# Half of the last attention placed between the second experts' products, in a four-layer transformer kernel

## The chip, the cores and the metric

The kernel runs on one core of a Trainium2 chip, as one program. The metric is the device time of that program in microseconds. A core has five engines that run side by side, each working through its own queue in order and waiting only for semaphores: TensorE (PE in the profile; its weight loads are PEld), VectorE (DVE), ScalarE (ACT), GpSimd (POOL), and SyncE (SP), which issues transfers. Matmul results land in PSUM, eight banks of 128 x 512 numbers; everything else lies in SBUF.

## What is computed

Four layers, each a cross-attention and a feed-forward, on x of 16 x 64 tokens with 128 features (1024 tokens, 8 tiles of 128). Every part reads the normalised x and adds its result to x. The part that matters here:

```python
x = x + L2_xattn(ctx, ctx, layernorm(x))          # deformable attention
x = x + L2_ffn(layernorm(x))                      # experts; only tokens 0..511 are routed
x = x + L3_xattn(layernorm(x), ctx, ctx, mask, bias)
x = x + L3_ffn(layernorm(x))

# L2_ffn: 8 experts, 128 -> 512 -> 128, two picked per token
h = gelu(ragged_dot(xs, w1, tokens_per_expert)); ys = ragged_dot(h, w2, tokens_per_expert)
out = zeros.at[tok].add(ys * weight) + bias

# L3_xattn: 16 heads of 8
q, k, v = clamp(Q @ Wq.T + bq), clamp(K @ Wk.T + bk), clamp(V @ Wv.T + bv)
logits = q @ k.T / sqrt(8) + clip(attn_bias, -1e4, 1e4)
logits = where(mask == 0, -1e4, logits)
x_add = softmax(logits) @ v @ Wo.T + bo

# L3_ffn: values rounded to a step of (largest of |v|) / 32767, five times one after the other
act_qdq(v) = clip(round(v / scale), ...) * scale,  scale = max(max|v| / 32767, 1e-12)
```

The expert picks come as inputs. Tokens 512 to 1023 get only the bias from L2_ffn, so after the deformable attention their x is complete up to that bias. The scale in act_qdq is the largest value of the whole tensor.

## The kernel before

There is no loop construct: the program is written out, engine by engine, in the order in which each queue runs it. "Tile j" is tokens 128 j to 128 j + 127.

*Deformable attention* (`deformable`, lines 1415 to 1936) works through 16 steps w. At its start ScalarE evacuates the offsets in two halves, and between them the two halves of the last layer's keys (lines 1550 to 1554), whose product TensorE has made at line 1389. VectorE then turns the first offsets to positions (`positions`, a chain of about 13 linked operations), GpSimd the other three quarters. At its end tokens 0 to 511 are finished first: context projection (w = 15), addition, statistics, and `HalfNorm`, a layernorm of one half of the tokens (lines 322 to 386). Tokens 512 to 1023 are finished between the experts (`late_half_pe`, `late_half_act`, `late_half_dve`).

*Second experts* (`moe2`, lines 1956 to 2033). For each of 8 experts TensorE makes four up products into PSUM banks 0 to 3 (line 2003), ScalarE applies GELU to each (line 2032), TensorE makes 16 down products into bank 4 or 5 by turns (line 2014), and VectorE adds the result, weighted per token, to x (line 1983, four instructions). TensorE's order is up(e + 1), down(e). Besides: the last layer's key guard (clamping; `guard`, lines 432 to 443), value products (line 492), value evacuation (line 457) and guard, key expansion to one copy per head group (line 451, VectorE), value spreading (line 481, ScalarE), and the limited bias, eight tiles (line 2093).

*Last attention* (`attention`, lines 507 to 739, masked). It begins when all x is done: layernorm of 8 tiles, query product in two halves (line 535), evacuation (543), guard of the queries, then 8 tiles in order 0 to 7. For a tile: scores on TensorE (585), times scale and plus limited bias on VectorE (686, 689), maximum (692), minus the maximum on GpSimd (667), exponential on ScalarE (645), clearing of NaN on VectorE (712), eight transposes on TensorE (599) and their evacuation on ScalarE (652), weighing of values and sums (612, 616), division on VectorE (718, 719, 723), output projection (636), addition (729) and statistics (251). TensorE runs scores one tile ahead and weighing two tiles behind.

*Last feed-forward* (`ffn3`, lines 2124 to 2327). Five times a largest value over all partitions is found and made a scale (`all_max`, lines 2156 to 2166), on which rounding on ScalarE and VectorE waits. The output leaves in two halves (line 2337).

`dve_link` makes VectorE wait for its own instruction; `stay_busy` issues matmuls whose result nobody reads.

## Time and profile before

| | us |
|---|---|
| time, median of 3 runs (502.0 to 504.98) | 503.25 |
| profiled execution, its own time | 501.5 |
| its span in the profile | 499.7 |
| TensorE busy (matmuls) | 398.9 |
| VectorE busy | 362.5 |
| ScalarE busy | 231.6 |
| GpSimd busy | 110.8 |

The span is from the first to the last instruction of the profiled execution; 1.8 us of its time lie around it. Busy times overlap, since the engines run side by side. The clock that TensorE was granted was 0.903 of full speed on average; it has two levels, 2.4 GHz (1.00) and 1.2 GHz (0.50).

### The profile page before, as it was taken

The numbers are of one execution on the slowest core, as the hardware profiler recorded it, in microseconds if no ns is written. First come the engines' busy times: TensorE is split into PE (matmuls) and PEld (weight loads), VectorE is DVE, ScalarE is ACT, GpSimd is POOL, SyncE is SP. The second block draws the span as 40 slices with busy tenths as digits, with TensorE's granted clock in tenths as the row PEclk, the third lists the DMA queues.
The fourth block names the chain that finished last, engine by engine and source line by source line (L and its number), as shares of the span: only waits on it lengthen the run. The fifth ranks groups of instructions, "written<-read, shape, count | busy, mean of one in ns | idle before, by whom it ended". The sixth has DMA issues, their size and how long they took to land.

```text
span 499.7 us, 8507 instructions
## 1 busy us (share of the span) xinstructions
PE 398.9 (80%) x3345; PEld 262.8 (53%) x3345; DVE 362.5 (73%) x806; ACT 231.6 (46%) x405; POOL 110.8 (22%) x95
## 2 busy tenths in 40 slices
PE   4998899999999887847888858999947386778155
PEld 2566565666566675623545434777742254653045
DVE  4889647567455779667788875198985999776974
ACT  3655663243222453437887857231712233343931
POOL 3100000009930010059925442000001343100000
PEclk9879999999999999988999987999976579679769
DMA  7960000000000000350000020000000000000001
GB/s 250 356 234 3 1 1 1 1 0 1 0 1 1 1 3 0 127 212 1 1 1 3 1 63 1 0 2 1 1 1 0 0 2 3 1 1 1 0 0 42
DMA packets 11068, 16.49 MB, mean 33 GB/s; under 512 B 5259, under 2 KB 9749, under 8 KB 10133
## 3 DMA queue, kind: packets, MB, share of 16 engines
q1 hardware_dynamic: 10740, 15.17, 8.6%
q10 hardware_dynamic: 288, 0.79, 0.4%
q8 instruction: 26, 0.43, 0.4%
q14 instruction: 14, 0.11, 0.1%
HBM read 15.43 MB, written 0.52 MB: 32 GB/s over the span
## 4 chain that ended last, share of the span: by engine, by line
PE 48%; DVE 35%; ACT 9%; issue 6%; DMA 1%; POOL 0%; ACTq 0%; DVEq 0%
PE ps L894 7%; PE ps L899 7%; PE ps L933 6%; PE ps L2003 4%; PE ps L2014 3%; PE ps L585 2%; DVE arena L689 2%; PE ps L1703 2%; DVE arena L686 2%; DVE arena L692 2%; PE ps L241 2%; DVE stats L251 2%; PE ps L1689 2%; PE ps L599 1%; DVE l2buf L2093 1%
## 5 line engine op out<-in xcount | busy, mean ns | idle before, releaser
L1012 DVE SCALAR_TENSOR_TENSOR arena<-ps,cols,arena 128x512 f32<-128x512 f32 x40 | 29.7, 750 | 42.3 <-PE ps L899 38.0
L908 ACT ACTIVATE arena<-ps,cols 128x512 f32<-128x512 f32 x40 | 27.4, 687 | 63.9 <-PE ps L894 63.8
L1838 DVE TENSOR_SCALAR arena<-ps 128x512 f32<-128x512 f32 x56 | 36.7, 684 | 10.0 <-PE ps L1689 5.6
L933 PEld LDWEIGHTS ps<-weights,arena 128*128 128x128 f32 x320 | 38.6, 192 | 8.1 <-issue 8.0
L933 PE MATMUL ps<-weights,arena 128*128 128x128 f32 x320 | 39.2, 276 | 0.2 <-DVE x_tm L1001 0.2
L899 PE MATMUL ps<-h_fm,weights 128*128 128x512 f32 x80 | 37.7, 594 | 0.7 <-DVE arena L1012 0.7
L894 PE MATMUL ps<-h_fm,weights 128*128 128x512 f32 x80 | 37.7, 594 | 0.6 <-ACT h_fm L382 0.6
L241 PE MATMUL ps<-const 128*128 128x256 f32 x114 | 29.9, 415 | 8.4 <-ACT arena L2243 4.6
L645 ACT ACTIVATE arena<-arena 128x1024 f32<-128x1024 f32 x16 | 16.9, 1057 | 37.3 <-POOL arena L667 29.9
L2003 PE MATMUL ps<-h_fm,weights 128*128 128x512 f32 x64 | 31.4, 639 | 0.7 <-ACT h_fm L382 0.7
L2014 PEld LDWEIGHTS ps<-weights,arena 128*128 128x128 f32 x256 | 29.7, 192 | 3.3 <-issue 3.1
L1689 PE MATMUL ps<-l2buf,picks_b 128*128 128x256 bf16 x160 | 26.9, 289 | 5.1 <-DVE arena L1838 3.7
L241 PEld LDWEIGHTS ps<-const 128*128 128x128 f32 x114 | 22.8, 208 | 14.5 <-ACT arena L2243 4.9
L599 PE MATMUL ps<-const,arena 128*128 128x128 f32 x128 | 23.1, 340 | 9.0 <-DVE arena L712 9.0
L2014 PE MATMUL ps<-weights,arena 128*128 128x128 f32 x256 | 29.7, 275 | 0.0
L2032 ACT ACTIVATE arena<-ps 128x512 f32<-128x512 f32 x32 | 18.6, 594 | 22.3 <-PE ps L2003 22.2
L585 PE MATMUL ps<-kexp,q_fm 32*64 32x256 f32 x256 | 25.5, 472 | 3.8 <-DVEq L552 1.9
L599 PEld LDWEIGHTS ps<-const,arena 128*128 128x128 f32 x128 | 18.7, 176 | 15.0 <-DVE arena L712 9.8
L667 POOL TENSOR_TENSOR arena<-arena 128x1024 f32<-128x1024 f32 x8 | 17.9, 2237 | 36.3 <-DVE arena L692 36.3
L899 PEld LDWEIGHTS ps<-h_fm,weights 128*128 128x128 f32 x80 | 15.1, 190 | 20.2 <-issue 18.2
L1703 PE MATMUL ps<-arena,kexp 128*32 128x320 f32 x256 | 20.5, 438 | 5.6 <-ACT l2buf L1784 4.1
L652 ACT ACTIVATE arena<-ps 128x512 f32<-128x512 f32 x32 | 17.9, 594 | 14.3 <-PE ps L599 14.3
(352 smaller groups left out, 837.3 us busy)
## 6 DMA issues: line engine op xcount, KB each, us to landing
weights<-in_moe_w SPq DMA_DIRECT2D x2, 2048.0 KB, 10.1
weights<-in_moe_w SPq DMA_DIRECT2D x3, 1280.0 KB
l2buf<-in_picks SPq DMA_DIRECT2D x1, 1664.0 KB, 7.5
rows<-in_rows SPq DMA_DIRECT2D x1, 1024.0 KB, 13.7
x_tm<-in_x SPq DMA_DIRECT2D x2, 256.0 KB, 4.9
ctx_fm<-in_ctx_fm ACTq DMA_DIRECT2D x1, 512.0 KB, 5.6
ctx_tm<-in_ctx SPq DMA_DIRECT2D x1, 512.0 KB, 14.5
mats<-in_mats SPq DMA_DIRECT2D x1, 512.0 KB, 14.6
```

The source lines that it names most:

```text
L241: PE.matmul(ps[:, bank, 0:256], ident, const[:, 0:256], start=True, stop=True)
L585: ins = PE.matmul(ps[64 * b:64 * b + 64, 2 * (t % 2) + g % 2, 256 * (g // 2):256 * (g // 2) + 256], q_fm[32 * g:32 * g + 32, t * P + 64 * ...
L599: ins = PE.transpose(ps[:, 4 + k, 128 * c:128 * c + 128], prob[j % 3][:, (4 * k + c) * 128:(4 * k + c + 1) * 128], ident)
L894: PE.matmul(ps[:, k, :], w1[:, e, P * k:P * k + P], h_fm[:, t], start=True, stop=True)\
L899: PE.matmul(ps[:, 2 + k, :], w2[:, e, P * k:P * k + P], h_fm[:, t], start=True, stop=True)\
L933: ins = PE.matmul(ps[:, 4 + u % 2, P * t:P * t + P], glu[:, u % 2, k, P * t:P * t + P], w3[:, e, k, :], start=(k == 0), stop=(k == 1))
L1012: V.scalar_tensor_tensor(out=glu[:, u % 2, k, :], in0=ps[:, 2 + k, :], scalar=bias_col(1, e, k), in1=silu[:, k, :], op0=ALU.add, op1=ALU.m ...
L1689: ins = PE.matmul(ps[:, m % 3, 256 * i:256 * i + 256], picks_b[:, 2 * c + i, :], ixm[:, hg, 256 * half:256 * half + 256], start=True, stop ...
L1703: ins = PE.matmul(ps[32 * hl:32 * hl + 32, 4 + par, 0:NK * S], kvc[:, j, 4 * hg + hl, :], hats[:, u % 2, NK * hl:NK * hl + NK, S * (2 * i ...
L1838: V.tensor_scalar(hat_rows(u, c), ps[:, m % 3, :], 0.0, 1.0, ALU.max, ALU.min).then_inc(near_ok, 1)
L2003: PE.matmul(ps[:, k, :], m2w1[:, e, P * k:P * k + P], h_fm[:, 0:T2], start=True, stop=True)\
L2014: ins = PE.matmul(ps[:, 4 + e % 2, P * j:P * j + P], hid[:, e % 2, k, P * j:P * j + P], m2w2[:, e, k, :], start=(k == 0), stop=(k == 3))
```

## The change

1. The last layer's keys are evacuated at the end of `int8_linear` and guarded before `positions`; its values are multiplied at the end of `deformable` (banks 0, 1, 2, 4) and evacuated there.
2. `last_keys_values`, `moe2` and the last call of `attention` are replaced by one function, `experts_and_last_attention`. In it up products rotate over three banks, down products use the single bank 3, tokens 512 to 1023 are normalised after accumulate(0), tiles 7, 6, 5 are attended between the experts, and tile 4 and then 3, 2, 1, 0 after them. ScalarE expands the keys. The limited bias is computed tile by tile. The output projection is done for groups of four, two, one and one tiles.
3. In `ffn3` the scale of each rounding is a step times a unit, so that the reciprocal follows the step directly; the output is in pieces of four, two and two tiles.

The helper functions inside the new function (scores, turn, weigh_values, logits, clear_nan, divide and so on) hold the same instructions as the old lines named above, for one tile.

```diff
--- before.py
+++ after.py
...
+        def keep_last_keys(act):
+
+            for k in range(2):
+                act.wait_ge(l3_keys[0], k + 1)
+                AC.activation(k_fm[:, 512 * k:512 * k + 512], ps[:, k, :], ACT.Identity,
+                              bias=col("L3_xattn_b_k")).then_inc(l3_keys[1], 1)
+
+        def guard_last_keys(dve):
+
+            dve.wait_ge(l3_keys[1], 2)
+            guard(k_fm[:], T, (l2buf[:, 5632:6656], l2buf[:, 6656:7680], wn[:].rearrange("p c i -> p (c i)")[:, 0:1024]))
+            keys_guarded.append(chained["dve"])
...
+        def keep_last_values(dve, g):
+
+            dve.wait_ge(v_ps, g + 1)
+            V.tensor_tensor(vdup[:, g], ps[:, VALUE_BANKS[g], :].rearrange("p (b e) -> p b e", b=4),
+                            over(row("L3_xattn_b_v"), 1, 4), ALU.add).then_inc(v_sb, 1)
...
+                keep_last_keys(act)
 
         int8_linear(3)
...
-                    if g == 0:
-                        for k in range(2):
-                            act.wait_ge(l3_keys[0], k + 1)
-                            AC.activation(k_fm[:, 512 * k:512 * k + 512], ps[:, k, :], ACT.Identity,
-                                          bias=col("L3_xattn_b_k")).then_inc(l3_keys[1], 1)
...
             def _(dve):
+                guard_last_keys(dve)
                 positions(dve, V, dve_link, 0, slice(0, 4), parts_ok)
...
                     if w == 15:
                         project_context(pe, 0, 3)
+                        last_values(pe, 0)
+                    if w == 16:
+                        last_values(pe, 1)
+                last_values(pe, 2)
+                last_values(pe, 3)
+                stay_busy(pe, 3, 5)
                 late_norm.turn(pe, 3)
...
                     if w == 16:
                         add_context(dve, 0, 3)
                         late_norm.moments(dve)
+                for g in range(4):
+                    keep_last_values(dve, g)
                 normalise(3)
...
+        def experts_and_last_attention():
...
+            TILES = (7, 6, 5, 4, 3, 2, 1, 0)
+            LATE = 4
+            GROUPS = ((4, 8), (2, 4), (1, 2), (0, 1))
+            GROUP_END = (4, 6, 7, 8)
...
+            SUM_BANK, O_BANK, Y_BANK = 3, 7, 3
+            early_rows, late_rows = HalfNorm(1), HalfNorm(0)
+
+            def score_banks(t):
+
+                return (0, 1) if t >= LATE and t % 2 == 0 else (4, 5)
+
+            def turn_banks(t):
+
+                return (2, 6) if t >= LATE else (6, 6)
...
+                def up(e):
+                    for k in range(4):
+                        n = 4 * e + k
+                        if n >= 3:
+                            pe.wait_ge(g_ok, n - 2)
+                        else:
+                            pe.wait_ge(v_sb, n + 1)
+                        PE.matmul(ps[:, n % 3, :], m2w1[:, e, P * k:P * k + P], h_fm[:, 0:T2], start=True, stop=True)\
+                            .then_inc(up_ps, 1)
+
+                def down(e):
+                    pe.wait_ge(g_ok, 4 * e + 4)
+                    if e >= 1:
+                        pe.wait_ge(sum_added, e)
+                    for j in range(4):
+                        for k in range(4):
+                            ins = PE.matmul(ps[:, SUM_BANK, P * j:P * j + P], hid[:, e % 2, k, P * j:P * j + P],
+                                            m2w2[:, e, k, :], start=(k == 0), stop=(k == 3))
+                    ins.then_inc(sum_ps, 1)
...
+                    j, banks = TILES[t], score_banks(t)
+                    if t == 0:
+                        pe.wait_ge(kx_ready, 1)
+                        pe.wait_ge(v_sb, 4)
+                        pe.wait_ge(q_ok, 1)
+                    if t == LATE:
+                        pe.wait_ge(kx_ready, 2)
+                        pe.wait_ge(q_ok, 2)
+                    for g in range(4):
+                        if g < 2 and t >= 1 and t != LATE:
+                            before = t - 1 if t < LATE else t - 2
+                            pe.wait_ge(sc_read, 2 * before + g + 1)
+                        if g >= 2:
...
+                def turn(t, k):
+                    if k == 0:
+                        pe.wait_ge(clean, t + 1)
+                    if t < LATE:
+                        if t + k >= 1:
+                            pe.wait_ge(pt_ready, 2 * t + k)
+                    elif t > LATE or k == 1:
+                        pe.wait_ge(pt_ready, 2 * (t - 1) + k + 1)
+                    for c in range(4):
+                        ins = PE.transpose(ps[:, turn_banks(t)[k], 128 * c:128 * c + 128],
+                                           prob[t % 3][:, (4 * k + c) * 128:(4 * k + c + 1) * 128], ident)
+                    ins.then_inc(ptT_ready, 1)
...
+                late_norm.wait_turned(pe)
+                pe.wait_ge(moe2_in, 64)
+                up(0)
+                up(1)
+                turn_late_context(pe, 6)
+                down(0)
+                project_late_context(pe, 7)
+                up(2)
+                down(1)
+                early_rows.turn(pe, 6)
+                up(3)
+                early_rows.wait_turned(pe)
+                queries(1, 7)
+                down(2)
+                scores(0)
+                up(4)
+                down(3)
+                scores(1)
+                up(5)
+                turn(0, 0)
+                down(4)
+                turn(0, 1)
+                up(6)
+                weigh_values(0)
+                turn(1, 0)
+                down(5)
+                turn(1, 1)
+                scores(2)
+                up(7)
+                down(6)
+                weigh_values(1)
+                turn(2, 0)
+                down(7)
+                scores(3)
+                turn(2, 1)
+                stay_busy(pe, 3, 2)
+                late_rows.turn(pe, 0)
+                weigh_values(2)
+                late_rows.wait_turned(pe)
+                queries(0, 1)
+                stay_busy(pe, 4, 2)
+                turn(3, 0)
+                turn(3, 1)
+                scores(4)
+                scores(5)
+                for t in range(5, NT + 3):
+                    if t + 1 < NT:
+                        scores(t + 1)
+                    if t - 2 < NT:
+                        weigh_values(t - 2)
+                    if t - 1 < NT:
+                        turn(t - 1, 0)
+                        turn(t - 1, 1)
+                    if t == 6:
+                        project(0)
+                    if t == 8:
+                        project(1)
+                    if t == 9:
+                        project(2)
+                    if t == 10:
+                        project(3)
...
+                pool.wait_ge(def_cx_ok, 2)
+                G.memset(v4[:], 0.0).then_inc(cleared, 1)
+                early_rows.wait(pool)
+                add_out_bias(slice(4, 8))
+                less_max(0)
+                less_max(1)
+                less_max(2)
+                late_rows.wait(pool)
+                add_out_bias(slice(0, 4))
+                for t in range(3, NT):
+                    less_max(t)
...
+                V.tensor_scalar(bqs[:, 1:2], col("L3_xattn_b_q"), 1.0, None, ALU.mult).then_inc(bq_ok, 1)
+                expert_gates()
+                late_norm.wait(dve)
+                dve_link(V.tensor_tensor(x_tm[:, 0:4], x_tm[:, 0:4], over(row("L2_ffn_bias"), 1, 4), ALU.add))
+                limits()
+                accumulate(0)
+                add_late_context(dve, 7)
+                early_rows.moments(dve)
+                limited_bias(0)
+                early_rows.factors(dve)
+                early_rows.apply_on_dve(dve, (0, 1))
+                guard_values(1)
+                accumulate(1)
+                limited_bias(1)
+                guard_queries(0, 1)
+                accumulate(2)
+                logits(0)
+                limited_bias(2)
+                accumulate(3)
+                logits(1)
+                clear_nan(0)
+                accumulate(4)
+                guard_values(0)
+                clear_nan(1)
+                limited_bias(3)
+                divide(0)
+                limited_bias(4)
+                accumulate(5)
+                logits(2)
+                limited_bias(5)
+                dve.wait_ge(vx_ready, 8)
+                limited_bias(6)
+                accumulate(6)
+                clear_nan(2)
+                limited_bias(7)
+                accumulate(7)
+                dve.wait_ge(sum_added, NE)
+                all_stats(range(0, 4))
+                late_rows.moments(dve)
+                divide(1)
+                late_rows.factors(dve)
+                late_rows.apply_on_dve(dve, (0, 1))
+                logits(3)
+                guard_queries(1, 0)
+                divide(2)
+                clear_nan(3)
+                logits(4)
+                for t in range(5, NT + 5):
+                    if t < NT:
+                        logits(t)
+                    if t - 1 < NT:
+                        clear_nan(t - 1)
+                    if 3 <= t - 3 < NT:
+                        divide(t - 3)
+                    if t == 7:
+                        add(0)
+                    if t == 8:
+                        add_stats(0)
+                    if t == 9:
+                        add(1)
+                    if t == 10:
+                        add(2)
+                        add_stats(1)
+                    if t == 11:
+                        add(3)
+                        add_stats(2)
+                    if t == 12:
+                        add_stats(3)
+                V.sem_inc(x_done, 1)
...
+                                            k_fm[:, 512 * k:512 * k + 512].rearrange("p (b k) -> p b k", b=8), ACT.Copy,
+                                            scale=const[:, C_HM + h:C_HM + h + 1])
+                    ins.then_inc(kx_ready, 1)
+
+                def spread_values(half):
+                    act.wait_ge(v_sb, 6 - half)
+                    act.wait_ge(cleared, V4_CLEAR_AGAIN)
+                    for part in range(4):
...
+                gelu(0)
+                gelu(1, (0, 1))
+                keep_late_context(act)
+                gelu(1, (2, 3))
+                keep_turned_late_context(act, 6)
+                spread_keys(1)
+                gelu(2)
+                early_rows.root(act)
+                early_rows.apply_on_act(act, (2, 3))
+                early_rows.keep_turned(act, 6)
+                gelu(3)
+                keep_queries(0, 1, 7)
+                spread_values(1)
+                gelu(4)
+                spread_keys(0)
+                exponential(0)
+                gelu(5)
+                keep_turned(0, 0)
+                exponential(1)
+                keep_turned(0, 1)
+                gelu(6)
+                keep_turned(1, 0)
+                spread_values(0)
+                keep_turned(1, 1)
+                gelu(7)
+                exponential(2)
+                keep_turned(2, 0)
+                late_rows.root(act)
+                keep_turned(2, 1)
+                late_rows.apply_on_act(act, (2, 3))
+                late_rows.keep_turned(act, 0)
+                keep_queries(1, 0, 1)
+                exponential(3)
+                keep_turned(3, 0)
+                keep_turned(3, 1)
+                for t in range(LATE, NT + 1):
+                    if t < NT:
+                        exponential(t)
+                    if t - 1 >= LATE:
+                        keep_turned(t - 1, 0)
+                        keep_turned(t - 1, 1)
+
+        experts_and_last_attention()
...
+            def set_unit(dve, i, ins):
+
+                dve_link(ins)
+                dve_link(V.reciprocal(least[:, i:i + 1], unit[:, i:i + 1]))
+                dve_link(V.tensor_scalar(least[:, i:i + 1], least[:, i:i + 1], 1e-12, None, ALU.mult))
+
             def all_max(dve, i):
 
 
                 dve.wait_ge(all_ps, i + 1)
                 dve_link(V.tensor_reduce(top, ps[:, 7, 0:P], AX.X, ALU.max))
-                dve_link(V.tensor_scalar(scl[:, i:i + 1], top, real[:, i:i + 1], 1e-12, ALU.mult, ALU.max))
-                dve_link(V.reciprocal(inv[:, i:i + 1], scl[:, i:i + 1]))
-
-                V.scalar_tensor_tensor(out=inv[:, i:i + 1], in0=inv[:, i:i + 1], scalar=32767.0, in1=real[:, i:i + 1],
-                                       op0=ALU.mult, op1=ALU.mult).then_inc(scale_ok, 1)
+                dve_link(V.tensor_scalar(step[:, i:i + 1], top, 1.0 / 32767.0, least[:, i:i + 1], ALU.mult, ALU.max))
+                V.reciprocal(inv[:, i:i + 1], step[:, i:i + 1]).then_inc(scale_ok, 1)
                 dve.wait_ge(scale_ok, i + 1)
+
+            def full_scale(i):
+
+                return V.tensor_tensor(scl[:, i:i + 1], step[:, i:i + 1], unit[:, i:i + 1], ALU.mult)
...
-                for k in range(2):
-                    for j in range(4 * k, 4 * k + 4):
+                for k, (j0, j1) in enumerate(PIECES):
+                    for j in range(j0, j1):
                         if j % 2 == 0:
...
                 for i in (GT, UP):
-                    ins = V.tensor_scalar(real[:, i:i + 1], scl[:, X:X + 1], 1.0 / 32767.0, None, ALU.mult)
-                dve_link(ins)
+                    set_unit(dve, i, V.tensor_copy(unit[:, i:i + 1], step[:, X:X + 1]))
...
                     if c == 0:
                         all_max(dve, UP)
+                        dve_link(full_scale(UP))
                     dve.wait_ge(dve_chain, product)
...
                 all_max(dve, GT)
-                V.tensor_scalar(real[:, GS:GS + 1], scl[:, GT:GT + 1], 1.0 / 65536.0 / 32767.0, None, ALU.mult)
+                dve_link(full_scale(GT))
...
+                set_unit(dve, GS, V.tensor_scalar(unit[:, GS:GS + 1], scl[:, GT:GT + 1], 1.0 / 65536.0, None, ALU.mult))
...
+                dve_link(full_scale(GS))
+                set_unit(dve, OUT, V.tensor_tensor(unit[:, OUT:OUT + 1], scl[:, GS:GS + 1], scl[:, UP:UP + 1], ALU.mult))
...
+                dve_link(full_scale(OUT))
+                for k, (j0, j1) in enumerate(PIECES):
...
+        PIECES = ((0, 4), (4, 6), (6, 8))
+        ffn3(5)
...
-            for k in range(2):
+            for k, (j0, j1) in enumerate(PIECES):
                 sp.wait_ge(halves_done, k + 1)
-                sp.dma_start(out.rearrange("(j p) d -> p j d", p=P)[:, 4 * k:4 * k + 4], x_tm[:, 4 * k:4 * k + 4])\
-                    .then_inc(out_done, 16)
-            sp.wait_ge(out_done, 32)
+                sp.dma_start(out.rearrange("(j p) d -> p j d", p=P)[:, j0:j1], x_tm[:, j0:j1]).then_inc(out_done, 16)
+            sp.wait_ge(out_done, 16 * len(PIECES))
...
```

## Rows read from the trace of the kernel before

**Rows 1.** Page, busy tenths of each engine in 40 slices of 12.5 us.

```profile
PE   4998899999999887847888858999947386778155
DVE  4889647567455779667788875198985999776974
```

**Rows 2.** Windows: start:end, length, busy us of PE, PEld, DVE, ACT, POOL, clock, DMA.

```profile
300.30:302.30 2.00, 1.16 (x5) 0.76 (x5) 0.86 (x2) 0.78 (x3) 0.00 (x0) 0.50 0.03 8
302.30:369.90 67.60, 64.23 (x396) 46.66 (x396) 49.45 (x89) 27.51 (x57) 3.51 (x1) 0.95 0.00 1
369.90:380.90 11.00, 5.59 (x12) 2.75 (x12) 5.80 (x25) 5.13 (x9) 2.36 (x1) 0.59 0.00 0
380.90:442.20 61.30, 39.67 (x592) 27.21 (x592) 54.24 (x85) 18.98 (x27) 17.90 (x8) 0.71 0.01 1
```

**Rows 3.** Chain that ended last: start us, us on it, what.

```profile
302.26 9.57 PE ps L2003 x16
...
322.84 0.89 PE ps L1649 x8
323.74 3.44 PE ps L2003 x8
327.17 3.57 PE ps L2014 x32
330.74 1.90 PE ps L492 x32
...
342.58 0.69 DVE l2buf L439
...
345.77 1.38 DVE l2buf L443
...
405.78 1.29 DVE arena L686 x2
```

**Rows 4.** Timeline, 200 to 334: start us, us, engine, line, names [idle before].

```profile
215.96 0.42 DVE L1568 TENSOR_TENSOR o_fm<-o_fm,const 128x256 f32<-128x256 f32 x1 [6.14 <-ACT o_fm L1548]
...
218.12 0.75 DVE L1573 TENSOR_TENSOR o_fm<-o_fm,sinv 128x256 f32<-128x256 f32 x1
...
300.46 1.11 PE L376 MATMUL ps<-const,h_tm 128*128 128x128 f32 x4 [4.21 <-ACT h_tm L358]
...
303.87 1.28 ACT L2032 ACT_TABLE_LOAD   x1
303.88 0.44 DVE L1881 TENSOR_REDUCE v<-v 128x32 f32<-128x160 f32 x1 [2.69 <-ACT v L1778]
...
305.16 0.60 ACT L2032 ACTIVATE arena<-ps 128x512 f32<-128x512 f32 x1
...
333.37 4.48 DVE L451 TENSOR_TENSOR kexp<-k_fm,const 128x2048 f32<-128x2048 f32 x2
```

**Rows 5.** Timeline of the last attention.

```profile
386.47 2.12 DVE L440 TENSOR_SCALAR ctx_tm<-q_fm 128x512 f32<-128x512 f32 x1
...
409.91 1.42 PE L585 MATMUL ps<-kexp,q_fm 32*64 32x256 f32 x16
...
410.41 0.95 DVE L719 RECIPROCAL arena<-arena 128x128 f32<-128x128 f32 x1
...
434.56 0.68 PE L612 MATMUL ps<-arena,v 128*32 128x64 f32 x31 [0.46 <-ACT arena L652]
...
435.07 0.64 PE L616 MATMUL ps<-arena,const 128*32 128x128 f32 x15
435.64 1.09 PE L599 MATMUL ps<-const,arena 128*128 128x128 f32 x8
```

**Rows 6.** Timeline of the last feed-forward.

```profile
468.49 0.16 DVE L2164 SCALAR_TENSOR_TENSOR arena<-arena 128x1 f32<-128x1 f32 x1
...
479.45 1.22 DVE L2310 SCALAR_TENSOR_TENSOR arena<-arena 128x1024 f32<-128x1024 f32 x1 [1.11 <-ACT arena L2243]
...
496.21 0.75 DVE L2325 SCALAR_TENSOR_TENSOR x_tm<-ps,arena,x_tm 128x512 f32<-128x512 f32 x1 [1.93 <-PE ps L2202]
```

463 lines of the change are left out of this document (239 added, 224 removed).

## The prediction

> **What bounds the kernel now.** The profile page comes first. In its 40 slices TensorE is dense and VectorE looser in slices 25 to 29, the second experts; in slices 31 to 35, the last attention, they change places [rows 1]. The stage windows put numbers on it [rows 2]. Experts, 302.3 to 369.9: TensorE busy 64.2 of 67.6 us, VectorE 49.5. Turn-over (layernorm, queries) to 380.9: 11.0 us in which neither is busy for much over half. Last attention to 442.2: VectorE 54.2 of 61.3, TensorE 39.7, much of that at a lower clock. So these are two stages one behind the other with different limits. Over both, 139.9 us, VectorE works 109.5 us and TensorE 109.5 us. The chain of waits says the same: TensorE up and down products with VectorE's accumulations at the end, then only VectorE logits [rows 3]. Tokens 512 to 1023 need no second experts, so their attention can fill VectorE's gaps there; tokens 0 to 511 can't, which is why it is half of the attention that moves.
>
> The timing is played through: four queues kept in order, durations from rows, each wait looked up.
>
> **Part by part: ahead of the experts.** Key evacuation moves to ScalarE's idle time before 207.9, the key guard to VectorE's idle 6.1 us before 215.96 [rows 4]. The guard is five operations, 342.58 to 347.15 = 4.6 us [rows 3]; it starts at 209.8 and ends at 214.4, so it costs nothing, with 1.5 us of cover left; without cover 4.6. The second offset evacuation then comes 1.3 us sooner, so GpSimd starts sooner beside VectorE's position chain, which is on the path. A product or sum of two 128x256 tiles took 0.42 us at 215.96 with GpSimd idle and 0.75 at 218.12 with it busy [rows 4]. Two or three more operations are caught: +0.6 (0 to 1.3).
>
> The first value product now lies between the context projection and the next turn on TensorE, on the chain: two groups of values take 1.90 us [rows 3], so +0.95. The other three and the stay-busy products fill TensorE's 4.2 us of idle before 300.46 [rows 4]. VectorE's four value evacuations, 4 x 0.69, fall where it waits 2.7 us for the exponential [rows 4], and the first up products wait for them, to 302.8, 303.6 and 304.3. The first GELU comes at 305.5 instead of 305.16 and there are three banks instead of four, so up(0) and up(1) end by GELU's pace at 310.5; before they ended at 311.8, since they ran at 1.2 GHz (granted 0.50 at 300.3 to 302.3 [rows 2], 9.57 us for 16 records, at full speed 2 x 3.44 [rows 3]). down(0) starts at 310.9: 0.7 us earlier.
>
> **Experts with three tiles inside.** TensorE's order from down(0) to the end of down(7): 8 downs x 3.57, 6 ups x 3.44, context projection 0.89 [rows 3], a turn of the norm 0.45, half the queries 0.86, scores of tiles 0 to 2 at 1.42, two weighings at 1.15, five half turns at 0.45 (eight transposes show 1.09, of which 0.2 is the last one's run-out) [rows 5]: 28.6 + 20.6 + 0.9 + 0.45 + 0.86 + 4.3 + 2.3 + 2.25 = 60.2. Without a stall down(7) would end at 371.2. With the queues in order I find these waits of TensorE: 0.5 for the norm rows, 1.6 for accumulate(1) (one sum bank; VectorE is in the value guard), 0.6 for guarded queries, 0.9, 1.6 and 0.9 for the cleared tiles 0, 1 and 2, and 0.5 of scraps: 6.6. down(7) ends at 377.8 and accumulate(7) at 379.1, against 369.8 before: the stage is 9.3 longer. VectorE has 109.5 less 4.5 (key expansion) less 4.6 less 2.8 (now ahead) = 97.6 us from 308.4 [rows 2 to 4], a floor of 406, so it can't be the bound before the late tiles.
>
> ScalarE takes the key expansion as 8 activations at 0.64 (the nearest row is a 128x512 GELU at 0.60 [rows 4]; a scale from a tile may add; bounds 0.60 and 0.75), 5 us. From the experts on it switches function tables 10 times instead of 3: GELU and exponential alternate. A switch costs 1.28 us: at 303.87 the load starts with the end of the exponential and GELU starts 0.01 us after it [rows 4]. 7 x 1.28 + 5 on 51.6 busy makes 66 of 130 us; most of it hides behind down products. The Trainium skill (ScalarE: Activation LUTs, "What ACT_TABLE_LOAD costs") adds a drain of about 1.38 us to each load and so budgets some 2.7 per switch, with the advice to group by table; this trace shows no such gap. By the page's price, played through the same queues, the end would come 6.5 us later, the sum would be 499.0.
>
> **Turn-over and the late tiles.** From accumulate(7): statistics, root and normalised rows 4.1 us, to 383.2; logits(3) 4.1; the query guard 4.9, since GpSimd's subtraction holds it up (0.42 became 2.12 at 386.47 [rows 5]); divide(2) and clear_nan(3) 2.2, to 394.4. By then TensorE has idled some 7 us, so its clock is low, as it was through much of the old attention (0.71 on average [rows 2]); two half turns and the scores of tile 4 take 4.1 before VectorE can start logits(4) at 398.5. From there it is the old loop: before, 405.78 to 442.2 = 36.5 from the first logits of tile 4 [rows 3]. Two of the seven divisions in it (reciprocal 0.95 [rows 5], 1.46 with the two small steps around it) are done already: 33.5. x_done comes at 432.0, against 442.2: **-10.2**.
>
> **Last layer.** Each scale drops one linked operation of 0.2 us [rows 6] ahead of the next step. Four of the five are on the chain (UP gets a product back): -0.8, of which I keep -0.6, since the linked operations added (set_unit three times two or three, full_scale) nearly fill the idle times that hide them, such as the 1.1 us ahead of 479.45 [rows 6]. The last output piece is half as large: some 0.4 instead of 0.75 on VectorE [rows 6], and 128 KB instead of 256 to land, -0.5. Sum -1.1 (+0.5 to -1.8).
>
> **Sum.** -10.2 + 0.6 - 1.1 = -10.7. The profiled execution, 501.5 with a span of 499.7, would be 490.8; against the median of 503.25 that is **492.5**.
>
> **Rivals.** *A, more stalls.* Sixteen hand-overs between TensorE, VectorE, ScalarE and GpSimd are inside the experts now, each in a fixed order, and mine count only 6.6 us. If each costs 0.4 more than the 0.05 us that I gave a semaphore, 6.4 us go: 499. For: no row of before shows such a mix of short steps. Against: the old experts, with eight hand-overs of their own, left TensorE idle 3.4 us of 67.6 [rows 2]. *B, more gain.* The tail keeps 2.4 GHz (the stay-busy products) and turns and scores stay short: 3 us off the turn-over and the last three tiles, and stalls of 4 instead of 6.6: 487. *C, slower.* The merged stage is TensorE-bound, and its waits could drop the clock to 1.2 GHz: an up product then takes twice its time, as most of the 9.57 us row does [rows 3]. Of the 67 us each microsecond of work at half speed costs one more; from 11 us on the gain is gone, and with a third of it (22 us) the time is 503.25 - 10.7 + 22 = 514. For: the last attention ran at 0.71. Against: there TensorE was busy 39.7 of 61.3 us and idle in long stretches, mine in the merged stage last at most 1.6, and the old experts had 0.95 [rows 2]. *E, dearer switches.* Each table load is followed by a stall as long as itself before ScalarE works on, and TensorE waits for the GELUs behind it: ten loads, 12.8 us more on ScalarE, about half of it passed on: 499. For: the order alternates GELU and exponential three times. Against: the 0.01 us behind the load at 303.87 [rows 4]. The page named above would make it so. *D, no change.* The 9.3 us by which the experts grow are repaid only if tiles 4 to 7 cost what they did; should each cost 2.7 us more, since their scores, turns and weighings stand in a new order at a low clock, nothing is left: 503. For: TensorE's order there is new. Against: VectorE's order, which sets the pace, is the old one.
>
> **Chances.** Forecast 0.58, B 0.13, A 0.13, E 0.04, C 0.06, D 0.06. A measurement of this kernel tells 0.5%, some 2.5 us, from no change. Of A I count 0.12 as faster, of E 0.03, the rest of both as the same; faster is 0.58 + 0.13 + 0.12 + 0.03 = 0.86, same 0.08, slower 0.06. The range reaches from B's 487 to between A and D, 501.
>
> **What would show it.** Right: accumulate(7) ends near 379 (sooner: my stalls are too many), granted clock above 0.9 from 305 to 379, logits(4) near 398, x_done near 432, the last layer 56 us. Ten or so table loads of 1.28 us each with no gap behind. Wrong: GELUs that wait for loads so that up products stand for over 2 us at a time, the position chain over 1 us longer, or a merged stage ending after 385.

## The result and the profile after

The changed kernel takes 491.76 us (median of four runs, 490.91 to 498.75) against 504.12 us: a ratio of 0.9747, 95% interval 0.9699 to 0.9795. The forecast was 492.5. One of the four runs (498.75) was in a slower state of the chip, and ratios are taken over the others. A second measurement gave 491.11 us, ratio 0.9735 (0.9688 to 0.9783). The profiled execution has a span of 489.7 us; before it was 499.7.

The page's 40 slices of the changed kernel answer to [rows 1]:

```profile
PE   3899889999999978874888888989988665778156
...
DVE  3879656558454687878688988997587959877985
...
PEclk9969999999999999997999999999999965978759
```

TensorE is at 8 or 9 tenths from slice 24 to 31 now, and VectorE at 7 to 9 except in slice 29. The gap behind is in slices 32 and 33 of TensorE and slice 33 of VectorE, and TensorE's clock falls in slices 33 and 34. The stage windows of the changed kernel answer to [rows 2]: the way to the experts, experts with three tiles inside, turn-over up to logits(4), four late tiles, last layer.

```profile
core 0: us, PE busy (x) PEld busy (x) DVE busy (x) ACT busy (x) POOL busy (x), PEclk, DMA share, GB/s
302.00:312.30 10.30, 8.40 (x25) 3.77 (x25) 9.86 (x25) 8.71 (x16) 0.59 (x1) 1.00 0.00 0
312.30:380.80 68.50, 63.61 (x501) 44.93 (x499) 55.71 (x93) 42.17 (x74) 13.22 (x5) 1.00 0.01 1
380.80:400.70 19.90, 11.02 (x108) 6.67 (x104) 13.97 (x30) 6.39 (x10) 3.29 (x2) 0.85 0.01 1
400.70:432.80 32.10, 20.71 (x328) 14.44 (x328) 28.62 (x47) 9.96 (x14) 8.74 (x4) 0.71 0.01 2
432.80:489.70 56.90, 34.88 (x126) 23.46 (x126) 43.13 (x97) 27.12 (x33) 0.00 (x0) 0.77 0.03 9
```

With three tiles inside, TensorE is busy 63.6 of 68.5 us at the full clock (1.00), and VectorE 55.7. The turn-over (from the last expert's sum to the first logits behind it) has become the loosest stretch: neither engine is busy for three quarters of 19.9 us. The late tiles are VectorE's, 28.6 of 32.1 us, as in [rows 2].

The timeline of the turn-over (start, duration, engine, line, operation; in brackets the idle time ahead and its releaser) has the points that the prediction named:

```profile
379.67 1.13 DVE L2199 SCALAR_TENSOR_TENSOR x_tm<-ps,arena,x_tm 128x128 f32<-128x128 f32 x4 [3.24 <-issue]
...
380.83 0.87 DVE L251 BATCH_NORM_STATS2 stats<-x_tm 128x6 f32<-128x128 f32 x4
...
384.53 1.28 DVE L2213 TENSOR_TENSOR arena<-ps,arena 128x512 f32<-128x512 f32 x2
...
388.68 0.43 DVE L1242 TENSOR_SCALAR arena<-q_fm 128x512 int32<-128x512 f32 x1
388.87 1.99 POOL L2140 TENSOR_TENSOR arena<-arena 128x1024 f32<-128x1024 f32 x1 [2.48 <-DVE arena L2219]
...
389.02 2.12 DVE L1243 TENSOR_SCALAR ctx_tm<-q_fm 128x512 f32<-128x512 f32 x1
...
394.64 0.68 DVE L2223 TENSOR_SCALAR arena<-arena 128x1024 f32<-128x1024 f32 x1
...
395.37 1.11 PE L2038 MATMUL ps<-const,arena 128*128 128x128 f32 x4 [5.79 <-DVE arena L2223]
...
400.70 1.29 DVE L2213 TENSOR_TENSOR arena<-ps,arena 128x512 f32<-128x512 f32 x2 [5.38 <-PE ps L2023]
```

accumulate(7) at 379.67, logits(3) at 384.53, the query guard from 388.68 with one operation stretched to 2.12 under GpSimd's 1.99 (as at 386.47 in [rows 5]), the clear at 394.64, then TensorE after 5.79 us of idling with 1.11 per four transposes, and logits(4) at 400.70.

**One mark for all kernels.** The executions arrive at the second half of the program at different times, from 207.0 to 211.7 us. Nothing ahead of it differs but the two key evacuations, which stand in ScalarE's idle time. So the table counts from the statistics of the norm ahead of the deformable layer (`BATCH_NORM_AGGREGATE`, from its row in each timeline) to its next ones: the late rows' norm, the end of accumulate(7), the first logits behind the experts (logits(0), or logits(4) where four tiles are ahead of them) and the last layer's norm; "last layer" is the span less that point.

```
kernel        mark    late norm  acc(7) end  first logits  x_done   last layer  median
before        207.00    90.0      162.8        175.4       235.3      57.4      504.1
before again  209.86    90.0      162.7        175.3       235.2      57.4      504.3
changed       208.39    91.2      172.4        192.3       224.5      56.8      491.8
again         208.30    91.2      172.4        192.3       224.5      56.8      491.1
apart         210.43    91.0      160.4        172.0       226.4      56.9      494.9
apart, guard  210.02    90.9      160.4        170.6       228.8      55.6      496.3
no GELU       211.60    91.2      171.9        192.0       224.2      57.0      491.3
values        207.60    90.0      172.3        192.2       224.4      56.4      489.9
filler        211.58    91.2      172.4        190.7       222.8      56.0      491.7
7 groups      208.06    91.2      172.4        192.3       224.5      55.5      490.2
tile 4        211.68    91.2      172.4        186.8       219.9      55.7      488.0
better        210.06    89.9      172.1        183.9       216.4      55.7      482.6
better 2      211.62    90.0      171.0        182.8       215.2      55.5      480.3
better 3      209.82    89.8      170.8        182.6       215.0      55.2      481.9
```

From the mark the stretches of two executions of one kernel agree within 0.2 us, where two medians of one kernel differ by up to 1.2. The mark itself goes with TensorE's clock, not with a kernel. The first `BATCH_NORM_AGGREGATE` behind 40 us comes at 49.6 to 52.6 us; from there to the mark it is 157.4 or 157.5 us in seven executions, 159.0 in the three in which the clock from 100 to 125 us was 0.96 or 0.97, and 160.7 in the four in which it was 0.91.

### The profile page after: what moved, and what is told of

The parts are those of the page before. It is cut to its first block, busy times and chain, and to the rows that moved or that the text cites. A ratio compares the mean times of both kernels' runs of the same rounds, so it can differ in the third digit from the quotient of the medians.

```text
span 489.7 us, 8572 instructions
## 1 busy us (share of the span) xinstructions
PE 401.0 (82%) x3365; PEld 262.0 (54%) x3365; DVE 365.2 (75%) x810; ACT 246.3 (50%) x423; POOL 112.7 (23%) x96
## 4 chain that ended last, share of the span: by engine, by line
PE 47%; DVE 34%; ACT 9%; issue 7%; DMA 1%; POOL 1%; POOLq 0%; ACTq 0%; DVEq 0%
PE ps L805 7%; PE ps L810 7%; PE ps L844 7%; PE ps L1999 3%; PE ps L1656 2%; PE ps L2023 2%; PE ps L241 2%; PE ps L496 2%; DVE stats L251 2%; PE ps L1642 2%; DMA ctx_fm<-in_ctx_fm 1%; DVE arena L1797 1%; PE ps L2497 1%; ACT arena L1733 1%; PE ps L2478 1%
## 5 line engine op out<-in xcount | busy, mean ns | idle before, releaser
L241 PE MATMUL ps<-const 128*128 128x256 f32 x134 | 36.3, 424 | 8.4 <-ACT arena L2538 4.4
L810 PE MATMUL ps<-h_fm,weights 128*128 128x512 f32 x80 | 37.7, 593 | 0.7 <-DVE arena L923 0.7
L805 PE MATMUL ps<-h_fm,weights 128*128 128x512 f32 x80 | 37.7, 594 | 0.6 <-ACT h_fm L382 0.6
L241 PEld LDWEIGHTS ps<-const 128*128 128x128 f32 x134 | 27.5, 213 | 15.9 <-ACT arena L2538 4.7
L1990 PE MATMUL ps<-h_fm,weights 128*128 128x512 f32 x64 | 30.1, 605 | 2.4 <-ACT arena L2326 1.5
L810 PEld LDWEIGHTS ps<-h_fm,weights 128*128 128x128 f32 x80 | 15.1, 190 | 20.2 <-issue 18.2
L2326 ACT ACTIVATE arena<-ps 128x512 f32<-128x512 f32 x32 | 18.2, 597 | 12.6 <-PE ps L1990 12.5
L1018 POOL TENSOR_TENSOR wn<-wn,winv 128x1152 f32<-128x1152 f32 x1 | 2.1, 2128 | 91.0 <-DVE winv L1008 91.0
L2140 POOL TENSOR_TENSOR arena<-arena 128x1024 f32<-128x1024 f32 x6 | 13.5, 2248 | 41.0 <-DVE arena L2219 41.0
L912 DVE SCALAR_TENSOR_TENSOR x_tm<-ps,arena,x_tm 128x128 f32<-128x128 f32 x80 | 22.4, 342 | 0.3 <-DVE stats L251 0.2
L1642 PEld LDWEIGHTS ps<-l2buf,picks_b 128*128 128x128 bf16 x160 | 13.1, 102 | 16.3 <-DVE arena L1797 9.7
L1990 PEld LDWEIGHTS ps<-h_fm,weights 128*128 128x128 f32 x64 | 11.3, 190 | 17.1 <-issue 10.7
L805 PEld LDWEIGHTS ps<-h_fm,weights 128*128 128x128 f32 x80 | 13.7, 191 | 10.4 <-issue 9.6
```

Of the source, the lines that this page charges most:

```text
L241: PE.matmul(ps[:, bank, 0:256], ident, const[:, 0:256], start=True, stop=True)
L805: PE.matmul(ps[:, k, :], w1[:, e, P * k:P * k + P], h_fm[:, t], start=True, stop=True)\
L810: PE.matmul(ps[:, 2 + k, :], w2[:, e, P * k:P * k + P], h_fm[:, t], start=True, stop=True)\
L912: ins = V.scalar_tensor_tensor(out=x_tm[:, j], in0=ps[:, 4 + u % 2, P * t:P * t + P], scalar=gates[:, j, e:e + 1], in1=x_tm[:, j], op0=ALU ...
L1642: ins = PE.matmul(ps[:, m % 3, 256 * i:256 * i + 256], picks_b[:, 2 * c + i, :], ixm[:, hg, 256 * half:256 * half + 256], start=True, stop ...
L1990: PE.matmul(ps[:, n % 3, :], m2w1[:, e, P * k:P * k + P], h_fm[:, 0:T2], start=True, stop=True)\
```

## The experiments

Ratios in brackets are to the kernel before, with their 95% intervals.

**The yardstick.** No edit.

> The changed kernel once more, as the yardstick for the kernels run beside it: 491 to 492.5 us, 12 to 13 below the kernel before (ratio .974 to .976). A theory by which the gain was the luck of one run would have the ratio above .98.

491.11 us, as expected.

**Attention and experts apart.** On all four queues the steps of tiles 7, 6, 5 and scores(3) move behind down(7); on TensorE, and likewise on the others:

```diff
                 down(2)
-                scores(0)
                 up(4)
                 down(3)
-                scores(1)
                 up(5)
-                turn(0, 0)
...
                 queries(0, 1)
                 stay_busy(pe, 4, 2)
-                turn(3, 0)
-                turn(3, 1)
-                scores(4)
-                scores(5)
-                for t in range(5, NT + 3):
+                scores(0)
+                scores(1)
+                for t in range(1, NT + 3):
```

> The changed kernel with all attention steps of tiles 7, 6, 5 and the scores of tile 4 moved behind the last expert (on all four engines); start, evacuation of keys and values, limits, queries of tokens 512 to 1023 between the experts, and the last layer stay as changed. Theory (the gain is the overlap): the merged stage loses some 12 us of TensorE work and 3 to 4 us of stalls, accumulate(7) near 367.5 in place of 379.7; the turn-over and eight tiles at 7.7 us behind it put x_done near 441.5 (changed kernel: 432.8), the time is 8 to 9.5 us longer: about 500.5 us, a ratio of .99 to .995 to the kernel before. Rival (the gain comes from what moved to idle times and from the last layer, the overlap is eaten by hand-overs): within 2 us of the changed kernel, 491 to 494. Rival C turned round (the merged stage pays a slower TensorE clock): accumulate(7) earlier than 364.

494.85 us (0.9821, 0.9771 to 0.9871): only 3.7 above the changed kernel by the medians and 1.9 counted from the mark. The theory missed by 5. (Apart from the order, the early tiles get the two alternating pairs of score banks and the two banks for transposes that the late ones have.) Its windows, experts, turn-over and eight tiles:

```profile
312.30:370.90 58.60, 55.68 (x332) 41.27 (x330) 41.31 (x83) 31.92 (x65) 5.96 (x2) 1.00 0.00 1
370.90:382.40 11.50, 6.42 (x39) 3.55 (x38) 4.77 (x18) 3.65 (x6) 1.26 (x1) 0.85 0.00 0
382.40:436.80 54.40, 35.08 (x575) 24.14 (x569) 50.37 (x77) 18.66 (x26) 17.86 (x8) 0.81 0.01 2
```

I had put 7.7 us on each of eight tiles, the old stage of 61.3 us over eight. It takes 54.4: a tile is 5.8 us of VectorE (logits start at 402.01, 407.83 and 413.66), and the rest of the old stage was not attention of tiles. The table gives the account of the overlap alone, apart against changed: the merged stage is 12.0 us longer (172.4 against 160.4), the turn-over 8.3 longer (19.9 against 11.6), and four tiles fewer behind it give back 22.2 (54.4 against 32.2). Left: 1.9.

**The guard put back.** The kernel apart with the guard of the early queries in the turn-over and the other behind the first logits:

```diff
                 limited_bias(1)
-                guard_queries(0, 1)
...
-                guard_queries(1, 0)
+                guard_queries(0, 1)
                 logits(0)
+                guard_queries(1, 0)
```

> The kernel with attention and experts apart, and in addition the query guard of tokens 512 to 1023 put back from the experts into the turn-over, with the guard of tokens 0 to 511 behind the first logits, where the kernel before has its second guard. Theory (the kernel apart gained on the kernel before by what was moved to idle times, mostly this guard, 2.6 us of work and 1.7 of contention in a stage that VectorE bounds, 386.14 to 390.5 before): first logits to x_done 54.4 + 4.3 = 58.7 us, the time 4 to 4.5 us above the kernel apart, 498 to 499. Rival (tiles are paced by GpSimd and ScalarE, the guard would fit between them): under 1.5 us.

496.32 us (0.9862, 0.9803 to 0.9922). From the first logits to x_done 58.2 in place of 54.4, +3.8 as the theory said (4.3), but the first logits no longer wait for the second half and come 1.4 sooner: net +2.4 from the mark to x_done (1.5 by the medians, and 1.1 to the end, since the last layer was 1.3 shorter in this execution). The theory was right on the guard and had left out what it released.

**GELU left out.** Here the experts' GELU is replaced by a function that changes nothing, so only the time counts.

```diff
-                        AC.activation(hid[:, e % 2, k, :], ps[:, n % 3, :], ACT.Gelu).then_inc(g_ok, 1)
+                        AC.activation(hid[:, e % 2, k, :], ps[:, n % 3, :], ACT.Identity).then_inc(g_ok, 1)
```

> The second experts use the identity in place of GELU (the GELU is left out), a function that no table load precedes anywhere in this trace, so the alternation of tables with the exponential is gone; four of the ten loads fall away and the exponentials' may with them. Theory (a switch costs its 1.28 us and no more, and half of the loads is passed on to TensorE as four waits of 1.1 to 1.4 us): accumulate(7) 2.5 to 4.5 us earlier, measured from the statistics of the deformable layer's norm, the time 487 to 489. Rival E (each switch costs about twice the load): 6 us or more off, below 485.5. Rival (the waits are absorbed, since TensorE would next wait for VectorE and the one sum bank): less than 1.5 us.

491.33 us (0.9744, 0.9686 to 0.9801), x_done 0.3 sooner from the mark. Of the ten loads from 302 to 382 us four are left, and accumulate(0) to (7) all come 0.5 to 0.6 us sooner: that is the first load ahead of a GELU, at 305.62, and nothing else. It delays ScalarE's copy ahead of GpSimd's clearing by 0.5 us, and VectorE's first limit ends 0.55 us behind the clearing in both kernels. Around up(5), first in the changed kernel, then without GELU:

```profile
344.19 1.06 ACT L2357 ACTIVATE arena<-arena 128x1024 f32<-128x1024 f32 x1
...
344.51 2.84 PE L1990 MATMUL ps<-h_fm,weights 128*128 128x512 f32 x6
...
345.71 1.28 ACT L2326 ACT_TABLE_LOAD   x1 [0.47 <-PE ps L1990]
...
347.01 1.57 ACT L2326 ACTIVATE arena<-ps 128x512 f32<-128x512 f32 x3
...
347.66 1.12 PE L1990 MATMUL ps<-h_fm,weights 128*128 128x512 f32 x2 [0.31 <-ACT arena L2326]
...
349.02 0.66 PE L2038 MATMUL ps<-const,arena 128*128 128x128 f32 x4 [0.24 <-DVE arena L2223]
```

```profile
346.87 1.06 ACT L2357 ACTIVATE arena<-arena 128x1024 f32<-128x1024 f32 x1
...
347.19 3.70 PE L1990 MATMUL ps<-h_fm,weights 128*128 128x512 f32 x8
...
348.41 0.60 ACT L2326 ACTIVATE arena<-ps 128x512 f32<-128x512 f32 x1 [0.49 <-PE ps L1990]
...
351.71 0.65 PE L2038 MATMUL ps<-const,arena 128*128 128x128 f32 x4 [0.82 <-DVE arena L2223]
```

The load starts where the first evacuation would, once the up product is there, and the GELU 0.02 us behind its end. The three banks let TensorE run ahead, so it waits 0.31, not 1.28, and up(5) takes 4.27 in place of 3.70. What it loses there it would lose on the next cleared tile: the transposes (L2038) wait 0.24 for it, and 0.82 without GELU. My theory (four waits handed on) falls, rival E more so: the rival of absorbed waits is what happens.

**Value products behind the loop.**

```diff
                     if w == 15:
                         project_context(pe, 0, 3)
-                        last_values(pe, 0)
-                    if w == 16:
-                        last_values(pe, 1)
+                last_values(pe, 0)
+                last_values(pe, 1)
                 last_values(pe, 2)
```

> The first two value products stand behind the loop of turns, with the other two, in place of between the context projection and the last turns. Theory of the prediction (one value product lies on the chain and costs .95, with the trace after 1.02): the norm's statistics of the late rows come .9 to 1.05 us sooner; the values then reach VectorE later but wait there anyway; down(0) .3 to 1.0 us sooner, the time .5 to 1.0 shorter, 490.3. Rival (the four products behind the loop now push the late rows' transposes and up(0)): the same time or up to 1 us longer.

The late rows' norm comes 1.2 us sooner (90.0 in place of 91.2), and at accumulate(7) 0.1 is left. The median is 489.93 us (0.9708, 0.965 to 0.9766), but from the mark, 207.6 in this execution, x_done comes only 0.1 sooner and the last layer is 0.4 shorter. The product was on the chain to the norm, as predicted, but that chain does not set the stage behind it; VectorE does, as the last experiments show.

**Filler in the turn-over.** `stay_busy(pe, 3, 2)` and `(pe, 4, 2)` become `(pe, 6, 2)` and `(pe, 16, 2)`.

> The changed kernel with more filler products in the turn-over: 6 and 16 groups in place of 3 and 4, so that TensorE is busy up to the transposes of tile 4. Theory (the turn-over loses to TensorE's 1.2 GHz): transposes .66 in place of 1.11, scores(4) 1.42 in place of 2.30, logits(4) 1.5 to 2.5 us sooner after the statistics of the deformable norm (192.3 there), the time 1.5 to 2 us shorter; the tiles behind are bound by VectorE and fall back to 1.2 GHz. Rival B of the prediction (the tail would keep 2.4 GHz too): 3 us or more. Rival (filler only queues ahead of the real products): 0 or up to 1 us longer.

The clock is 0.98 in place of 0.85 up to logits(4):

```profile
386.00:402.20 16.20, 13.82 (x124) 9.77 (x123) 12.07 (x19) 5.91 (x9) 3.28 (x2) 0.98 0.01 2
402.20:434.40 32.20, 21.77 (x335) 15.45 (x329) 28.61 (x48) 10.05 (x14) 8.74 (x4) 0.69 0.01 2
```

logits(4) comes 1.6 us sooner, x_done 1.65: the theory's price of the half clock (1.5 to 2.5), at its low end. The late tiles fall back to 0.69 and take 32.2 us as ever. The median (491.71; 0.9748, 0.9683 to 0.9813) shows nothing of it; its profiled execution started at 211.58.

**Fewer filler groups in the last layer.** `stay_busy(pe, 10, 5)` becomes `(pe, 7, 5)`. VectorE's row for the last maximum, changed kernel, then this one:

```profile
476.87 0.16 DVE L2610 TENSOR_REDUCE arena<-arena 128x1 f32<-128x3 f32 x1
...
478.94 0.29 DVE L2454 TENSOR_REDUCE arena<-ps 128x1 f32<-128x128 f32 x1 [1.92 <-PE ps L2467]
```

```profile
476.55 0.16 DVE L2610 TENSOR_REDUCE arena<-arena 128x1 f32<-128x3 f32 x1
...
477.29 0.29 DVE L2454 TENSOR_REDUCE arena<-ps 128x1 f32<-128x128 f32 x1 [0.58 <-PE ps L2467]
```

> In the last layer 7 in place of 10 filler groups ahead of the last maximum. Theory (the filler queue of 6.89 us, issued at 471.79, ends 1.3 us after the maximum's operand is there and delays it): L2454 follows L2610 by 1.1 us in place of 2.07, time .8 to 1.0 us shorter, about 490.8. Rival (the filler keeps the clock up: 6.89 us of it against 6.03 before show a falling clock already): the products behind it (L2497) take 6.5 to 8 us in place of 5.67 and the time is the same or up to 1.5 us longer.

490.24 us (0.9725, 0.9672 to 0.9778), the last layer 1.4 shorter. The wait with ten groups is 1.07 to 2.37 us over the kernels here (before: 1.13), and it goes with the time that the ten groups take: 6.03 us before, 6.04 in the kernel with tile 4 earlier (wait 1.07), 6.89 in the changed kernel (1.92). So this last layer, the same in all kernels with ten groups, takes from 55.6 to 57.0 us.

**Tile 4 one slot earlier.**

```diff
                 weigh_values(1)
+                scores(3)
                 turn(2, 0)
                 down(7)
-                scores(3)
...
                 queries(0, 1)
                 stay_busy(pe, 4, 2)
+                scores(4)
                 turn(3, 0)
                 turn(3, 1)
-                scores(4)
...
                 clear_nan(2)
-                limited_bias(7)
+                logits(3)
                 accumulate(7)
...
-                logits(3)
-                guard_queries(1, 0)
                 divide(2)
+                limited_bias(7)
+                guard_queries(1, 0)
                 clear_nan(3)
```

> Tile 4 goes one slot earlier: its scores before the transposes of tile 5, its logits between clear(2) and accumulate(7) where VectorE stood idle 3.24 us, its subtraction ahead of GpSimd's wait for the late rows; limited_bias(7) and divide(2) move into the turn-over, scores(4) before the transposes of tile 4. Theory (the turn-over is a VectorE chain: logits(3) 4.1, guard 4.9, divide and clear 2.2, then a TensorE wait of 5.8): accumulate(7) at 379.7 to 380.5, logits(4) near 393.5 in place of 400.7, x_done near 426.5, time 485 to 486.5. Rival 1 (VectorE is full, the logits only push accumulate(7)): accumulate(7) near 382, gain 1.5 to 3 us, 488.5 to 490. Rival 2 (the tiles behind are bound by the half clock of TensorE after the turn-over, not by where they start): within 1 us of the changed kernel.

488.01 us (0.9663, 0.9612 to 0.9715). accumulate(7) does not move (172.4): the logits took only VectorE's idle 3.24 and the place of a limited bias. logits(4) comes 5.5 sooner, x_done 4.5, since the late tiles take 33.1 in place of 32.2. The theory was 1.8 short of its 6.3: VectorE now stands 3.55 us ahead of divide(2), for weigh(2) behind the late rows' transposes at half clock, and the limited bias stands between that and the guard. (On GpSimd less_max(3) moves ahead of its wait for the late rows, which the lines above do not show.)

**Better kernels.** Tile 4, value products, 7 groups, 8 and 8 groups of filler in the turn-over, and

```diff
-                late_rows.turn(pe, 0)
                 weigh_values(2)
+                late_rows.turn(pe, 0)
...
-                divide(2)
                 limited_bias(7)
+                divide(2)
                 guard_queries(1, 0)
```

> Tile 4 one slot earlier, 7 filler groups in the last layer, value products behind the loop, and in the turn-over: weigh(2) ahead of the late rows' transposes, limited_bias(7) ahead of divide(2), 8 and 8 groups of filler in place of 3 and 4 so that TensorE keeps 2.4 GHz. Theory, against the changed kernel: tile 4 -4.5 (measured from the norm of the deformable layer), last layer -1.4, values -.9, turn-over -2 to -3: the time 481.5 to 483.5. Rival (the turn-over stays bound by the chain accumulate, norm, queries, guard, and filler helps nothing): 484 to 485.5.

482.61 us (0.9557, 0.951 to 0.9604), in the theory's range: from accumulate(7) to logits(4) 11.8 us in place of 19.9, TensorE's clock 1.00 in it. That is about as short as in the kernel apart (11.6).

The second takes GpSimd off VectorE:

```diff
-                pool.wait_ge(def_cx_ok, 2)
-                G.memset(v4[:], 0.0).then_inc(cleared, 1)
-                early_rows.wait(pool)
-                add_out_bias(slice(4, 8))
                 less_max(0)
                 less_max(1)
+                early_rows.wait(pool)
+                add_out_bias(slice(4, 8))
...
                 keep_queries(0, 1, 7)
+                act.wait_ge(def_cx_ok, 2)
+                AC.activation(v4[:].rearrange("p (i c) -> p i c", i=16), over(const[:, 0:256], 1, 16), ACT.Copy,
+                              scale=0.0).then_inc(cleared, 1)
                 spread_values(1)
```

> The better kernel with GpSimd taken off VectorE's back at the start of the second experts: the clearing of the expanded values (3.5 us on GpSimd at 312, under which the first limit takes 3.68 in place of .68) becomes a ScalarE copy of some 4.2 us in ScalarE's idle time of 4.75 us ahead of gelu(4), and the output bias of tokens 512 to 1023 is added after less_max(1). Theory (VectorE is solid from 300 to 337 and sets accumulate(0) and (1)): accumulate(0) 3.0 and accumulate(1) 1 to 3.5 us sooner, accumulate(7) 1 to 2.5 us sooner, the time 480 to 481.5. Rival (TensorE is the bound of the merged stage, 64.4 of 68 us busy): accumulate(7) less than .7 us sooner, the time 482 to 483.

The first limit with GpSimd's clearing beside it (changed kernel), then without:

```profile
311.71 3.51 POOL L2147 MEMSET v<- 128x4096 f32 x1 [11.36 <-ACT l2buf L1611]
...
312.14 3.63 DVE L2183 TENSOR_SCALAR arena<-arena 128x1024 f32<-128x1024 f32 x1
```

```profile
315.15 0.69 DVE L2181 TENSOR_SCALAR arena<-arena 128x1024 f32<-128x1024 f32 x1
```

480.32 us (0.9544, 0.949 to 0.9597), the fastest median here. From the mark accumulate(0) comes 2.3 sooner, accumulate(7) 1.1: between theory and rival. VectorE loses its 2.9 us, but TensorE is busy 66.3 of 69.9 in the stage of the better kernel and has no more to give.

The third adds filler in the late tiles:

```diff
+                    if t in (5, 6):
+                        stay_busy(pe, 3, 3)
                     if t - 1 < NT:
                         turn(t - 1, 0)
```

> As the run before, and three groups of filler behind the weighings of tiles 4 and 5, so that TensorE keeps 2.4 GHz in the late tiles (it falls at 396 in the better kernel and comes back at 413). Theory: scores(5) to (7) and the turns at full speed, .5 to 1.5 us less from logits(4) to the end of the attention (32.4 us). Rival (VectorE sets the pace): the same within .3 us, or up to 1 us longer where filler at 1.2 GHz stands ahead of transposes.

From logits(4) to x_done 32.4 in both, 481.92 us (0.955, 0.95 to 0.9601). The filler raised TensorE's clock in this stretch only from 0.77 to 0.84, not to 1.00. As far as it goes the rival holds: VectorE, busy 28.7 and 28.8 us of it, sets the late tiles' pace.

**The kernel before, a second profile.** No edit.

> The kernel before once more, with a second profile. The pair of profiles shows 10 us between before and after, the medians 12 to 13. Theory (the profile of before caught an execution in which TensorE's clock was granted in full up to 207 us; in others it is granted .91 to .97 somewhere from 60 to 125 us and all that follows comes up to 3.5 us later): its profile, if over 503 us, shows the statistics of the deformable norm at 209 to 211 in place of 207.0 and 235 us from there to the end of the attention, as before. Rival (before varies in its last attention, at a low clock): the norm at 207 and a longer stretch behind it.

504.29 us, profiled 504.18 with the mark at 209.86, 235.2 us from it to x_done and 57.4 behind, both as before. TensorE's clock in the first 50 us was 0.86 in this execution (as in the better kernel, mark 210.1) and 0.90 in the other; where it was 0.91 from 100 to 125 us (tile 4, no GELU, filler, better 2), the mark was 211.6 or 211.7. The three windows are of before again, tile 4 and the changed kernel:

```profile
0.00:50.00 50.00, 41.31 (x509) 25.46 (x510) 35.41 (x82) 25.39 (x49) 6.10 (x7) 0.86 0.59 210
```

```profile
100.00:125.00 25.00, 25.00 (x110) 16.24 (x109) 14.99 (x34) 7.75 (x10) 8.84 (x4) 0.91 0.00 1
```

```profile
100.00:125.00 25.00, 25.00 (x113) 15.44 (x112) 15.72 (x34) 9.12 (x12) 12.12 (x6) 1.00 0.00 1
```

The theory held, with the dip earlier than expected.

## Why the prediction was right

Point by point, less the 1.4 us by which this execution reached the mark later:

- **Start.** The value product costs 1.2 (0.95 predicted); down(0) starts 0.7 earlier, as predicted. GpSimd beside the position chain costs 0.3, not 0.6: on the raw clock the chain is 1.45 us behind before at L1520, 2.56 at L1536 and 1.72 behind it, at L1586. So the sign of being wrong (over 1 us) was touched inside the chain and not at its end. The 0.6 was added to x_done all the same, where none of it is left. What the prediction did not see is that the product's 1.2 is absorbed by VectorE later (0.1 is left of it at accumulate(7)).
- **Merged stage.** accumulate(7) starts at 379.67, 378.3 on the clock of before; its end, 379.4, was put at 379.1. TensorE idled 4.9 us of the window (68.5 less 63.6), not 6.6; of its 63.6 us some 1.3 are scores(3), so up to down(7) it worked 62.3, not 60.2. Stalls 1.7 too high, work 2.1 too low: the end fits to 0.3 us because two errors cancel, which is luck. Rival C is out, the clock is 1.00 throughout; so is rival E: ten loads, as predicted, with 0.01 or 0.02 us behind one, and the loads that come with GELU cost the kernel 0.3 to 0.6 in all. The Trainium skill (ScalarE: Activation LUTs, "What ACT_TABLE_LOAD costs") adds a drain to each load; this trace does not agree.
- **Turn-over.** logits(4) at 399.3 on the clock of before, 398.5 predicted; guard, clear and half clock came as listed. The half clock's part is 1.6 us (filler), and most of logits(3), 4.1 us, could have been hidden (tile 4).
- **Late tiles.** 33.5 from logits(4) predicted, 32.2 measured. The old loop had an addition and a statistic in each tile (0.28 + 0.28, behind 411.61), the new one does them in groups; I had taken the old pace over.
- **Last layer.** -0.6, not -1.1. The scales gained their share, but ten filler groups at TensorE's lower clock held the last maximum back by 0.8 more than before (1.92 against 1.13).
- **Sum.** From the mark to the end 292.7 before and 281.3 after: -11.4, where -10.7 was predicted (-9.6 of it up to x_done, -10.2 and +0.6, and -1.1 in the last layer; measured -10.8 and -0.6). The late tiles and the position chain came out better, the turn-over and the last layer worse. The two profiled spans differ by only 10.0, because that execution of before had an early mark; the medians show 12.4, and the 1.0 over the 11.4 is within their scatter. In rival C, 503.25 - 10.7 + 22 is 514.6, not 514.

The number was right, and so was the order of the steps, each within 1.5 us, but the prediction let its reader believe that the overlap makes the gain. The experiments split the part up to x_done, 10.8: the overlap 1.9 and the guard out of the tiles 2.4. The last layer's 0.6 is read from the stage alone, and its clock moves it by more than that from kernel to kernel (55.6 to 57.0). The other 6.5 are what the kernel apart with its guard put back has over the kernel before: the experts' stage from the late norm to accumulate(7) 3.3 shorter (72.8 against 69.5, of which 1.8 is there when down(0) starts: keys on ScalarE, values and limits in gaps, first products at full clock), the turn-over 2.4 shorter (norm and products of four tiles instead of eight), the tiles 1.7 (grouped additions), the start 0.9 longer. None of these was tried alone: by the stages they are where the two traces differ, and which step of the change gives how much is open.

Why so little from the overlap: TensorE was the bound inside the experts, and 12 us more of work and stalls lengthened it by 12 us (from 102.0 us behind the mark on, busy 65.5 of 70.4 us against 55.5 of 58.4); the same work lay hidden under VectorE in the old stage. Each tile moved saves 5.8 of VectorE and costs some 3.6 of TensorE (12.0 us over three tiles and the fourth's scores), and the turn-over, which took in the fourth tile's logits, its guard and the half clock, took the rest. That is the price of this turn-over and not of every overlap: in the better kernel it is 11.8 us, about as in the kernel apart, and x_done comes at 216.4 in place of 226.4. No run has attention apart with the same repairs, so how much of those 10.0 us is the overlap's stays open.

## What to carry to other kernels

When work moves from a stage bound by one engine into a stage bound by another, it saves the first engine's time and costs the second's: count both, per tile, before the move (here 5.8 against 3.6). Put into the stage only what fills an idle row (VectorE's 3.24 us ahead of accumulate(7) took logits(3), once a limited bias of 1.22 had made room), and look at the turn-over behind, which nobody owns: here 8 of 20 us went with a reorder and filler. And undo a large change by parts: the part that gave it its name was a sixth of the gain here, with the turn-over behind it as it first was.

## What was not expected of the hardware

- A 128x4096 clearing on GpSimd holds a VectorE operation of 0.69 us for 3.63: the two hardly overlap at all. Without GELU the clearing ends 0.5 us sooner from the mark, and the operation takes 3.09: it ends 0.55 us behind the clearing both times. ScalarE does the same clearing in 3.61 us, and VectorE's operations beside it take what they took without it (0.43 us for this one):

```profile
333.44 3.61 ACT L2377 ACTIVATE v<-const 128x4096 f32<-128x4096 f32 x1
...
333.69 0.43 DVE L1242 TENSOR_SCALAR arena<-q_fm 128x512 int32<-128x512 f32 x1
```

- TensorE's granted clock differs between executions of one program even where it is busy without a break (0.91 or 1.00 in 100 to 125 us, busy 25.00 of 25.00), and with it all that follows comes 3.2 us later. A pair of profiles is compared from a common mark, not from zero.
